# Two Fourier layers on one core: loads divided between the queues of SyncE and ScalarE, VectorE alone empties PSUM in the mixing stage

## The reference

```python
# layer 1, the one whose mixing is changed
x_ft = jnp.fft.rfft2(xt, s=(M, N)) / scale_fwd
a = x_ft[:, :, :nm, :nm]                 # nm = 32
blk1 = _complex_matmul_2d(a, fw1)        # fw1, fw2: (64, 64, 32, 32, 2) float32
blk2 = _complex_matmul_2d(a, fw2)
out_ft = out_ft.at[:, :, :nm, :nm].set(blk1)
out_ft = out_ft.at[:, :, N - nm:, :nm].set(blk2)
out = jnp.fft.irfft2(out_ft, s=(N, M))
```

## Time and profile before

| | us |
|---|---|
| median of 3 runs (lowest, highest) | 2583.09 (2573.79, 2587.32) |
| the profiled execution's own time | 2586.72 |
| its span in the trace | 2584.9 |

### The profile page before, as it was taken

One profiled execution on the slowest core, in us unless ns is written; L12 is line 12 of the kernel. 1 busy time (PEld: TensorE's weight loads), 2 busy tenths in 40 slices (PEclk: granted clock), 3 DMA queues, 4 the chain that ended last, 5 costly groups with the idle time before them and its releaser, 6 DMA issues. The chain is left out here.

```text
span 2584.9 us, 60445 instructions
## 1 busy us (share of the span) xinstructions
PE 1920.0 (74%) x24234; PEld 1537.6 (59%) x24234; DVE 1411.0 (55%) x2087; ACT 1145.1 (44%) x1884; POOL 194.5 (8%) x218
## 2 busy tenths in 40 slices
PE   4788887888389233323453699989999989999999
PEld 3566665667357232323343577777877777777877
DVE  5665665664144300000352576677777767777876
ACT  4544454553023200000232565556666556555665
POOL 0000000000100310110001120200102020201000
PEclk9999998999555555555676899999999999999999
DMA  7777676772664999999654487887878788878887
GB/s 274 237 221 221 222 229 204 231 238 87 153 83 67 193 232 232 233 234 223 168 179 176 130 285 261 286 287 238 279 255 302 257 288 271 294 267 266 275 285 274
DMA packets 239409, 590.30 MB, mean 228 GB/s; under 512 B 67302, under 2 KB 159938, under 8 KB 202306
## 3 DMA queue, kind: packets, MB, share of 16 engines
q1 hardware_dynamic: 203266, 570.90, 74.1%
q10 hardware_dynamic: 35072, 12.59, 2.4%
q0 software_dynamic: 768, 2.56, 0.3%
HBM read 380.99 MB, written 168.30 MB: 212 GB/s over the span
## 5 line engine op out<-in xcount | busy, mean ns | idle before, releaser
L1257 ACT ACTIVATE x_turned<-ps_xt 128x512 f16<-128x512 f32 x512 | 305.7, 597 | 422.8 <-PE ps_xt L1345 422.8
L1300 DVE TENSOR_TENSOR x_turned<-ps_xt,x_turned 128x512 f16<-128x512 f32 x512 | 350.6, 685 | 188.4 <-ACT x_turned L1257 169.9
L1389 PE MATMUL ps_y<-apply,x_turned 128*128 (+1 forms) x6144 | 436.5, 222 | 0.0
L1389 PEld LDWEIGHTS ps_y<-apply,x_turned 128*128 128x128 f16 x6144 | 385.9, 99 | 67.9 <-issue 5.2
L1345 PE MATMUL ps_xt<-c_eye,x_in 128*128 128x128 f32 x2048 | 321.6, 281 | 81.0 <-DMA x_in<-in_x 55.9
L221 DVE TENSOR_TENSOR parts<-stage,parts 128x1024 f16<-128x1024 f32 x256 | 304.3, 1220 | 127.5 <-ACT parts L145 126.8
L1321 DVE SCALAR_TENSOR_TENSOR y_out<-ps_y,relu 128x512 f32<-128x512 f32 x512 | 350.6, 685 | 30.2 <-PE ps_y L1389 12.7
L1267 ACT ACTIVATE relu<-ps_wave 128x512 f32<-128x512 f32 x512 | 303.1, 592 | 21.2 <-PE ps_wave L1375 21.1
L291 PE MATMUL row_ps<-parts,c_rows_dft 128*64 128x512 f16 x1536 | 215.2, 421 | 125.5 <-DVE parts L221 119.1
L145 ACT ACTIVATE parts<-stage 128x1024 f16<-128x1024 f32 x256 | 255.2, 1049 | 74.6 <-issue 37.2
L1345 PEld LDWEIGHTS ps_xt<-c_eye,x_in 128*128 128x128 f32 x2048 | 222.8, 144 | 84.8 <-DMA x_in<-in_x 45.7
(11 more groups left out here) (117 smaller groups left out, 2053.6 us busy)
## 6 DMA issues: line engine op xcount, KB each, us to landing
stage<-in_x SPq DMA_DIRECT2D x256, 512.0 KB, 4.6
x_in<-in_x SPq DMA_DIRECT2D x128, 1024.0 KB, 9.4
out_y<-y_out SPq DMA_DIRECT2D x128, 1024.0 KB, 4.8
fw_first<-in_fw SPq DMA_DIRECT2D x16, 2048.0 KB, 22.5
fw<-in_fw SPq DMA_DIRECT2D x16, 2048.0 KB, 24.7
raw<-mixed SPq DMA_DIRECT2D x16, 1024.0 KB, 6.8
planes_in<-planes SPq DMA_DIRECT2D x8, 1536.0 KB, 15.2
fw_first<-in_conv SPq DMA_DIRECT2D x8, 1024.0 KB, 16.0
```

What stands on the lines that cost most here:

```text
L1257: nc.scalar.activation(turned[u % 2][:, 0, :, :], ps_turn[u % 2][:, :, :], ACT.Copy).then_inc(turn_high, 1)
L1300: nc.vector.tensor_tensor(v[:, 1, :, :], ps_turn[u % 2][:, :, :], v[:, 0, :, :], ALU.subtract).then_inc(turn_split, 1)
L1389: mm = nc.tensor.matmul(ps_y[u % 2][:, :, 2 * k:2 * k + 2], turned[u % 2][:, p, k, :], apply[:, bass.ds(b, 1), q, :, :].rearrange("p o c w ...
```

## The change

1. norm_0: SP issues the 8 loads into partitions 0 to 63 alone; ScalarE issues the 8 into partitions 64 to 127 at the start of its program.
2. mixing_1: SP issues the halves `f` = 0 and ScalarE the halves `f` = 1 of the weight loads. VectorE empties all banks, with one semaphore `taken` in place of two. ScalarE issues the 16 stores of a chunk together, when the chunk is emptied, and executes nothing else.
3. project_1: the loads of images 2 to 7 are issued by ScalarE, at step 1 of image `b` for image `b` + 2; those of images 0 and 1 stay with SP.

```diff
@@ norm_0, SyncE
                 sp.dma_start(xm[0:C, b, :, :, :], modes_x[b]).then_inc(modes_landed, 16)
-
-                sp.dma_start(xm[C:, b, 0:K0, :, :], modes_x[b, :, 0:K0]).then_inc(modes_landed, 16)
@@ norm_0, ScalarE
+            for b in range(B):
+                act.dma_start(xm[C:, b, 0:K0, :, :], modes_x[b, :, 0:K0]).then_inc(modes_landed, 16)
@@ mixing_1
+        def load(eng, f, n):
+            chunk, part = divmod(n, PASSES)
+            if n >= SL:
+                eng.wait_ge(ready, (n - SL + 1) * KC)
+            eng.dma_start(fw_slot(weights[n % SL], f), fw_chunk(fw[f], chunk * KC * 2 * K1, part)
+                          ).then_inc(landed[n % SL], 16)
 
         @block.sync
-                sp.wait_ge(taken_even, ((chunk + 1) * CHUNK_STEPS + BANKS) // 2)
-                sp.wait_ge(taken_odd, ((chunk + 1) * CHUNK_STEPS + BANKS) // 2)
+                sp.wait_ge(taken, (chunk + 1) * CHUNK_STEPS + BANKS)
...
+        @block.scalar
+        def _(act):
+            def store(chunk):
+                act.wait_ge(taken, (chunk + 1) * CHUNK_STEPS + BANKS)
+                for k in range(KC):
+                    t, x = divmod(chunk * KC + k, TURN)
+                    at, q = K1 // TURN - (x > 0) - t, -x % TURN
+                    for j in range(4):
+                        act.dma_start(mixed[1, :, :, at, j * MG:(j + 1) * MG, q, :].rearrange("b r y w -> (b r) y w"),
+                                      out[chunk % 2][32 * j + R // 2:32 * j + R, :, k, :]).then_inc(stored_1[chunk % 2], 16)
+            for n in range(1, SL):
+                load(act, 1, n)
+            for chunk in range(CHUNKS_1):
+                for n in range(chunk * PASSES + SL, (chunk + 1) * PASSES + SL):
+                    if n < LOADS:
+                        load(act, 1, n)
+                store(chunk)
@@ mixing_1, VectorE
-                        for k in range(1, KC, 2):
+                        for k in range(KC):
@@ project_1, SyncE
-                if b + 2 < B:
-                    sp.wait_ge(combined, 4 * (b + 1))
-                    load(b + 2)
@@ project_1, ScalarE
+                if s == 1 and b + 2 < B:
+                    act.wait_ge(combined, 4 * (b + 1))
+                    load(act, b + 2)
                 act.wait_ge(out_ready, n + 1)
```

More of the change, by code:

```diff
@@ L773, in mixing_1 @@
         ready = m.sem("mix1_ready")
-        taken_even = m.sem("mix1_taken_even")
-        taken_odd = m.sem("mix1_taken_odd")
+        taken = m.sem("mix1_taken")
         stored_0 = [m.sem(f"mix1_stored_0{i}") for i in range(2)]
@@ L802, in _ @@
             for n in range(1, SL):
-                load(n)
+                load(sp, 0, n)
             for chunk in range(CHUNKS_1):
@@ L810, in _ @@
                 sp.wait_ge(stored_0[i], 64 * (CHUNKS_1 // 2) + 1)
+        @block.scalar
[15 more added lines that the diff above has]
+                store(chunk)
+            for i in range(2):
+                act.wait_ge(stored_1[i], 64 * KC * (CHUNKS_1 // 2) + 1)
         @block.gpsimd
@@ L842, in _ @@
                                 pe.wait_ge(placed, 2 * (t * TURN + i * KC + k + 1))
-                            pe.wait_ge((taken_even, taken_odd)[k % 2], t * (TURN * PASSES // 2) + step // 2 + 1)
+                            pe.wait_ge(taken, t * (TURN * PASSES) + step + 1)
                             for g in range(MG):
@@ L856, in quadrants @@
             return [slice(32 * j, 32 * j + R) for j in range(4)] if R < 32 else [slice(0, P)]
[L858 to L888, removed]
         @block.vector
         def _(dve):
-            dve.sem_inc(taken_odd, BANKS // 2)
+            dve.sem_inc(taken, BANKS)
             for i in range(2):
+                dve.sem_inc(stored_0[i], 1)
                 dve.sem_inc(stored_1[i], 1)
@@ L905, in _ @@
                                                              ps[step % BANKS][rows, :, :])
-                            last.then_inc(taken_odd, 1)
+                            last.then_inc(taken, 1)
 PROJECT_SCALE = 1.0 / (N * float(np.sqrt(np.float32(N * (N // 2 + 1)))))
@@ L946, in out_slots, with load @@
             return [out[b % 2][:, h, part, :, q:q + STEP, :] for part in range(2)]
+        def load(eng, b):
+            v = raw[b % 2]
+            for f in range(2):
+                src = mixed[f, b].rearrange("r x y q w -> (x y) r (q w)")
+                eng.dma_start(v[:, f, :, 0:Q - 1, :, :].rearrange("p r k o w -> p r (k o w)"),
+                              src[0:P]).then_inc(landed[b % 2], 16)
+                eng.dma_start(v[0:K1, f, :, Q - 1, :, :].rearrange("p r o w -> p r (o w)"),
+                              src[P:, :, 0:2 * C]).then_inc(landed[b % 2], 16)
         @block.sync
         def _(sp):
[L950 to L957, removed]
             for b in range(min(B, 2)):
                 sp.wait_ge(cleared, b + 1)
-                load(b)
+                load(sp, b)
             for b in range(B):
-                if b + 2 < B:
-                    sp.wait_ge(combined, 4 * (b + 1))
-                    load(b + 2)
                 sp.wait_ge(out_taken, (b + 1) * STEPS)
```

## The result

The changed kernel takes **2518.1 us** (median of 4 runs, 2515.45 to 2519.81) beside 2583.24 us for the kernel before (4 runs on the same chip): a ratio of 0.9752, with a 95% interval of 0.9724 to 0.978. The profiled execution took 2518.0 us, its span is 2516.2.

A forecast was written before the change was run, and what follows sets the result against it. Mixing was taken as bound by transfers: SP's never-idle queue loads one half of the partitions at a time, near 200 GB/s. -69 - 8 - 10 = -87 on 2586.7 gives 2500, as a median 2495; range 2460 to 2535.

The forecast's parts named there:

- The half of the partitions is the limit: Mixing's weight loads: about 200 GB/s goes with writing only 64 partitions; one queue takes the two halves one after the other.
- two queues share one limit: Rival, 9%: 197 GB/s belongs to memory reads or DMA engines; a chunk stays 45.6 us, only project_1 gains, 2573 us.
- Mixing, -69: Mixing stage: chunks fall from 45.6 to 36.7 us, 62 us, plus 7 us at load 1; bounds -38 and -95.
- (b): Mixing, the chunk time chosen: all traffic, 10.5 MB, at 286 GB/s takes 36.7 us.
- (c): Mixing, slow bound: pairs of halves at 286 GB/s, 14.7 us a load, then 11.8 us of stores alone; 41.1 us a chunk.
- ScalarE's own issuing: Mixing: the next load waits behind issuing 8 stores, up to 11 us, while TensorE still has 12.9 us of work.
- if ScalarE's queue runs dry while its issuing engine stands at a wait: One of two conditions under which the prediction was said to fail; no size given.
- Evictions by VectorE alone, nothing: Mixing: four evictions of 692 ns a load, 2.8 us beside TensorE's 12.9, cost no time.
- norm_0, -8: norm_0: modes' halves load together, 8.3 MB at 307 to 401 GB/s, VectorE goes on earlier; bounds -5 and -11.
- project_1, -10: project_1: raw loads leave SP's queue, an image takes 14.5 to 15 us instead of 17.5; bounds -19 and +8.
- ScalarE's queue as the longer one: Rival, 5%, mixing: shared limit, ScalarE's stores without loads beside them; 54.4 us a chunk, 2635 us; slower under 230 GB/s a pair.

The follow-up runs named there:

- r5: Changed kernel with both queues loading the same half of the partitions together, first `f` = 0, then `f` = 1: 2573.78 us, ratio 0.9884, mixing_1 355.6 us.
- r6: Changed kernel with the 16 stores of a chunk in mixing_1 issued by GpSimd instead of ScalarE: 2484.29 us, ratio 0.9604.
- r9: The changed kernel once more, with no edit: 2523.6 us, ratio 0.9764, mixing_1 327.6 us.
- r8: The kernel before, with VectorE alone emptying the banks of mixing_1 and nothing else changed: 2583.67 us, ratio 0.9988.
- r7: Changed kernel with GpSimd's stores of zeros in norm_0 held back until the modes have landed: 2518.03 us, ratio 0.975.
- r12: r6 with r7's wait, and four of an image's eleven stores in project_1 issued by GpSimd: 2482.4 us, ratio 0.9609.

## Why the prediction was right, and where not

The forecast was 2495, the range 2460 to 2535, the result 2518.1: faster, by the named mechanism, within the range, and 23 us less than said. Point by point:

- **The half of the partitions is the limit: shown for the weights.** Only their source tensor, which changes with the half, is not told apart from it. r5 against the changed kernel, 195 to 207 against 340 GB/s, and 355.6 against 326.2 us. The rival that two queues share one limit falls. The Trainium skill ("DMA: Bandwidth & Descriptors", rules for kernel authors) says that transfers to disjoint halves serialize; 340 against 207 GB/s go against it here, and the measurement decides. The rule on the DMA port swizzle (the Trainium skill, "SBUF — State Buffer", section on the DMA port swizzle) agrees in size. Which ports are used, still no row shows.
- **Mixing, -69: right in kind, mis-sized; measured -38.** The wrong term is the chunk's 36.7 us, bound (b), which measured 40.5, near (c) with 41.1. Not the rate was too low: a pair of halves moved at 340, better than assumed. What failed is the reason for taking (b), that ScalarE's stores can have company in SP's free time. In the queue that also carries a half of every load they held that half back: from the third chunk on the half in `fw_first` landed 9.8 to 13.4 us behind SyncE's. r6 puts the stores into a third queue and has 36.6 us a chunk, which is (b), and a stage of 298.7, nearly the 296 forecast. ScalarE's own issuing was costed at up to 11 us for 8 stores, covered by TensorE's 12.9; there are 16 behind one another, and they took 31.4. That is a part of the delay; its share is open (r9). The clause "if ScalarE's queue runs dry while its issuing engine stands at a wait" does not describe it: the engine stood in its stores, and the queue was without a packet for 13 of 280 us.
- **Evictions by VectorE alone, nothing: right** (r8).
- **norm_0, -8: measured -3, outside its bounds of -5 and -11.** The term is the joint rate: 307 to 401 was taken, 284 came. r7 shows that the zeros cost 2.8 us of the wait, and that without them the rate is 245, so the modes don't double by halves as the weights do. Why not, stays open.
- **project_1, -10: measured -3, inside -19 and +8.** The wait for raw data went as forecast, 31.4 us to 8.0, and ScalarE's gaps at its four issues are 1.2 to 1.7 us, not 3. But ScalarE's wait for stores rose from 12.7 to 43.9 us. The mis-sized term is the image beside raw loads: 14.5 to 15 us was taken, 16.7 came, so four images gain 4 x (17.5 - 16.7) = 3.2 us. The 12.85 us of stores with nothing beside them was the wrong price for stores beside loads. r12 shows that the stores were what was left: divided, -17 us.
- **ScalarE's queue as the longer one, slower than before: half of it.** It was the longer one (13 us without a packet, SP's 39), but a pair of halves is far above the 230 GB/s under which that would make the kernel slower. It cost gain and no more.
- **The sum.** By touched stages -44.5, not -87. The total is 65 below before, as some 10 us came from pass_2, which no step foresaw, and the rest, as far as the traces tell, from a pass_1 whose length varies by 27 us among them. With the touched stages alone 2539 would have come out, just over the range. The range held partly by luck.

## What to carry to other kernels

When a load-bound stage shows about half of the best rate of its own trace, look at which partitions the transfers write: loads for both halves under way at once gave 340 GB/s instead of 200, two queues on one half gave nothing. Then issue both halves in the same moment, and keep trains of small stores off the engines and queues that carry them; here that train held back 27 us more, beside the 38 that the second path had brought. And sum a prediction by stages: with no line changed in them, pass_1 lies between 653.6 and 680.8 us and pass_2 between 1165.9 and 1182.1.

## What the hardware showed that was not expected

An engine that issues behind weight halves in its own queue is held up: 16 stores of 64 KB took ScalarE 31.4 us, 12.56 of them for the first, which takes 0.36 when no half is ahead. GpSimd, with no loads in its queue, issued the same stores at 529 ns each. The DMA share of a window does not tell whether there is room: it stood at 1.14 for 207 GB/s, and at 1.09 for 340. And the modes' halves reached only 245 GB/s together, where the weights reached 340, through the same two queues.
